# Attention with a mixture of experts on one Trainium2 core: products three periods behind the scores instead of four, with four buffers for the blocks that TensorE turns

## The chip, the cores and the metric

The kernel runs on one core of a Trainium2 chip. The metric is the device time of one execution in microseconds. The kernel before took 584.26 us, the median of three runs (584.21 to 585.72).

## The reference

The input x has 2 batches of 1024 tokens with 128 features, in f32. It is layer-normed, and the output is x plus an attention branch plus a mixture-of-experts branch, both of the normed x:

```python
q = xn @ wq.T                      # 16 heads of 64
lat = xn @ w_down.T                # 64 latent features, shared by all heads
k, v = lat @ w_k_up.T, lat @ w_v_up.T
q, k = rope(q), rope(k)
probs = softmax(q @ k.T / 8 + causal)      # [2, 16, 1024, 1024]
attention = (probs @ v) @ wo.T
```

The experts are 16 of width 64, of which each token uses four (chosen by groups), and one shared expert of width 256.

## The kernel before, in words

All five engines have programs written out by hand, with semaphores between them. The kernel has a first part (layer norm, routing, experts, up to about 126 us) and then the attention loop, which is what the change touches.

**Units and periods.** A unit is one batch and four heads (8 units, `UNITS`). Each unit has 8 periods, so there are 64 (`GRPS`). Period k deals with one pair of heads (a = 0 and 1) and two row blocks of 128 queries: a long one (8, 7, 6 or 5 key blocks) and a short one (1, 2, 3 or 4 key blocks). The two together are always nine key blocks. The work of a period is spread over iterations of the loops `for k in range(-1, GRPS + LAG + 1)`, which every engine runs in its own form. In what follows, iteration i is the pass of that loop with k = i.

**TensorE**, in iteration i, does in this order:
- `long_scores(i + 1)`: scores of the long rows of the next period,
- `project(i - LAG - 1)`: 8 small matmuls that take the products of a period to the 128 output features,
- `turn_slow(i)`: 8 transposes of those probability blocks that TensorE turns itself,
- `rotary`: one piece of q or k for a later unit,
- `short_scores(i + 1)`,
- `products(i - LAG)`: 36 matmuls, latent rows by turned probabilities.

With `LAG = 4` the products of period k stand at the end of iteration k + 4.

**Two ways to turn the probabilities.** The products need each 128x128 block of probabilities transposed. The first five blocks of each long row (`FAST = 5`) are turned by VectorE in 32x32 squares (`turn_fast`, tile `zig`) and then put in place by DMA (tile `fastT`). The other four blocks per head (`SLOW = 4`) are turned by TensorE (`turn_slow`) and copied by ScalarE from PSUM to one of `SLOTS = LAG + 1` buffers `slowT` (`copy_slow`, which waits for the products of period k - SLOTS).

**The exchange.** The DMAs that put the squares in place are issued by SyncE for two periods at a time, pair j being periods 2j and 2j + 1. `exchange(j)` waits until VectorE has turned both periods, and until the products of period 2j - 3 are done, so that the buffer `fastT[j % 2]` is free; it then issues 16 DMAs of 80 KB:

```python
sp.wait_ge(zig_done, 4 * j + 4)
if j >= 2:
    sp.wait_ge(pv_done, 2 * (j - 1))
```

SyncE reaches `exchange(j)` in its own loop at k = 2j + 1. The same queue also issues `stack(n, p)`, 4 DMAs of 256 KB that bring the rotated q and k of unit n into place: `stack(n, 0)` in front of the exchange of k = 8n - 3 (pair 4n - 2), and `stack(n, 1)` in front of the exchange of k = 8n - 1 (pair 4n - 1). The first half of the output is stored by the same queue, at k = GRPS // 2 + LAG + 3.

**Who waits for the exchange.** `products(k)` waits for `in_fast`, the landing of all 16 DMAs of its pair. For an even period k = 2j this is the first use of the pair. On TensorE, everything of the next iteration is queued behind that wait. `turn_fast` on VectorE waits for the exchange of two pairs earlier before it writes over `zig`.

**ScalarE**, in iteration i, does `scale_rows(i - LAG - 1)`, the exponentials of the long rows of i + 1, `copy_slow(i)`, `copy_output(i - LAG)` and the exponentials of the short rows of i + 1. **GpSimd** adds the scaled result of period i - LAG - 1 to the accumulator and rotates q and k.

Of the kernel before, what the change touches and what calls it, by code (L numbers as in the profile page):

```python
# [29 lines left out]

LONG, SHORT = [7, 6, 5, 4], [0, 1, 2, 3]
RING = 8
LAG = 4
SLOTS = LAG + 1
PAIRS = 2
GRPS = 4 * PAIRS * UNITS
# [51 lines left out]
def block_kernel(nc, x, wq, w_down, w_kup, w_vup, wo, gate, e_up, e_down, s_up, s_down,  # L88
                 c_rope, c_ident, c_mask, c_sel, c_lower, out):
    ctx = ExitStack()  # L90
    with ctx:
# [115 lines left out]
        def _(sp):  # L207
# [22 lines left out]
            def exchange(j):  # L230

                s = j % 2
# [3 lines that stand above are left out]
                for turn_ in range(4):  # L236
                    for qi in range(4):
                        ki = (qi + turn_) % 4
                        sp.dma_start(fastT[s][32 * ki:32 * ki + 32, qi],  # L239
                                     zig[s][32 * qi:32 * qi + 32, ki]).then_inc(in_fast[s], 16)  # L240
# [6 lines left out]
            for k in range(-1, GRPS):  # L247
# [8 lines left out]
                if k >= 0 and k % 2:  # L256
                    exchange(k // 2)
                if k == GRPS // 2 + LAG + 3:
                    sp.wait_ge(ad_done, GRPS)
# [9 lines left out]
        def _(pe):  # L269
# [120 lines left out]
            def long_scores(k):  # L390
                if k:
                    pe.wait_ge(max_done, 4 * k)
                if k % 4 == 0:
                    pe.wait_ge(in_qk[pair_of(k)], STACK * (unit_of(k) + 1))
                for chunk in range(2):
                    scores(k, 0, chunk)
# [32 lines left out]
            def project(k):  # L429
                m0 = unit_of(k) % QUADS * 2 + pair_of(k)  # L430
                pe.wait_ge(o_done, k + 1)
                pe.wait_ge(rope_dve, min(k + LAG + 1 + LATER, PIECES * UNITS))
                for c in range(2):
                    for a in range(2):
                        half = slice(HD * a, HD * a + HD)
                        last = nc.tensor.matmul(ps[:, 7 - a, c * P:(c + 1) * P],  # L436
                                                oT[k % 2][half, c * P:(c + 1) * P], mix[half, m0, :],
                                                start=True, stop=True)
                        if c == 1:
                            last.then_inc(proj_pe, 1)  # L440
# [32 lines left out]

            for k in range(-1, GRPS + LAG + 1):
                if 0 <= k and k + 1 < GRPS:
                    long_scores(k + 1)
                if k >= LAG + 1:
                    project(k - LAG - 1)
                if 0 <= k < GRPS:
# [424 lines left out]
```

## Time and profile before

| | |
|---|---|
| median of three runs | 584.26 us |
| the profiled execution | 588.68 us |
| its span, first to last instruction | 586.9 us |
| mean granted TensorE clock, of full speed | 0.971 |
| TensorE matmul busy | 537.9 us (92%) |
| VectorE busy | 407.8 us (69%) |
| ScalarE busy | 398.0 us (68%) |
| GpSimd busy | 194.0 us (33%) |
| moved by DMA | 66.52 MB, mean 113 GB/s |
| DMAs of the exchanges | 512 of 80 KB, 2.1 us from issue to landing (median) |
| DMAs of the stacks | 64 of 256 KB, 4.3 us |

Times within the profile are counted from the first instruction of the profiled execution. A busy share is an average over the whole span; the views by stretch and by time tell what an engine does in one stretch. SPq is the queue of SyncE: its rows are the issuing of DMAs, the transfer itself comes after.

### The profile page before, as it was taken

Reading aid. Unit: us, or ns where it says so; the run is one execution under the profiler, and the core shown is the slowest. Engines: PE = TensorE matmul, PEld = TensorE weight load, DVE = VectorE, ACT = ScalarE, POOL = GpSimd, SP = SyncE. Lnnn points to the kernel's source line nnn. Section 1 sums busy time; section 2 is a strip of 40 time slices with the busy share of each in tenths; the row PEclk is TensorE's granted clock in tenths of the full one; section 3 lists DMA queues with packets and bytes.
Section 4 is the critical chain, followed back from the end, with each engine's and each line's share of the span. In section 5 each row is a group of like instructions: output and inputs, shape, how many; then the busy total and the mean of one; then the engine's idle time right before and its main releaser. Section 6 shows DMA issues by size and latency. Waiting matters only on the chain.

```text
span 586.9 us, 13821 instructions
## 1 busy us (share of the span) xinstructions
PE 537.9 (92%) x4914; PEld 395.9 (67%) x4914; DVE 407.8 (69%) x921; ACT 398.0 (68%) x1036; POOL 194.0 (33%) x271
## 2 busy tenths in 40 slices
PE   3899999986899999999999999999999999898864
PEld 2657776753477777777777777777777776666663
DVE  5495537358877887878788878878877887676400
ACT  2364222347577887888788788878877888888722
POOL 3004404001144443344443344433443432122121
PEclk9599999998899999999999999999999999999977
DMA  9400004202366447646654764466556646654331
GB/s 280 119 1 2 0 1 94 50 2 61 96 157 164 112 99 162 152 108 142 154 138 113 162 163 120 97 151 154 150 137 154 145 118 158 156 126 118 96 86 36
DMA packets 41620, 66.52 MB, mean 113 GB/s; under 512 B 13632, under 2 KB 20688, under 8 KB 41424
## 3 DMA queue, kind: packets, MB, share of 16 engines
q1 hardware_dynamic: 38992, 64.20, 45.8%
q10 hardware_dynamic: 2560, 1.45, 0.8%
q8 instruction: 39, 0.64, 0.5%
q14 instruction: 29, 0.24, 0.1%
HBM read 5.84 MB, written 1.05 MB: 12 GB/s over the span
## 4 chain that ended last, share of the span: by engine, by line
PE 73%; DVE 10%; SPq 7%; issue 5%; ACT 3%; DMA 1%; DVEq 0%; POOLq 0%; POOL 0%; ACTq 0%
PE ps L386 23%; PE ps L425 21%; DVE prob_l L772 6%; SPq L239 6%; PE ps L410 5%; PE ps L451 5%; PE ps L469 4%; PE ps L332 3%; PE ps L436 3%; PE ps L302 1%; PE ps L453 1%; DMA acc<-x 1%; SPq L227 1%; PE ps L348 1%; PE ps L367 1%
## 5 line engine op out<-in xcount | busy, mean ns | idle before, releaser
L772 DVE CUSTOM_DVE_ANT_0 prob_l<-ps,mask 128x1024 f32<-128x1024 f32 (+3 forms) x128 | 126.0, 1022 | 86.7 <-PE ps L386 86.7
L386 PE MATMUL ps<-qk 64*128 64x512 f32 (+3 forms) x768 | 161.1, 524 | 19.8 <-DVE negmax L772 18.6
L593 ACT ACTIVATE prob_l<-prob_l,negmax 128x1024 f32<-128x1024 f32 (+3 forms) x128 | 126.1, 999 | 14.7 <-DVE negmax L772 14.7
L855 POOL TENSOR_TENSOR acc<-acc,scaled 128x256 f32<-128x256 f32 x128 | 93.4, 730 | 124.9 <-ACT scaled L496 119.9
L846 POOL TENSOR_TENSOR roped<-prod 128x256 f32<-128x256 f32 x64 | 46.5, 727 | 221.3 <-DVE prod L663 221.3
L386 PEld LDWEIGHTS ps<-qk 64*128 64x128 f32 x768 | 64.1, 187 | 79.7 <-issue 44.5
L785 DVE STREAM_TRANSPOSE zig<-prob_l 128x640 f32<-128x640 f32 x128 | 100.2, 821 | 1.4 <-DMA fastT<-zig 1.4
L496 ACT ACTIVATE scaled<-ps,rden 128x128 f32<-128x128 f32 x256 | 73.0, 368 | 41.6 <-PE ps L436 41.6
L425 PEld LDWEIGHTS ps<-fastT,lat 128*64 128x64 f32 x1280 | 70.6, 139 | 32.7 <-issue 31.0
L425 PE MATMUL ps<-fastT,lat 128*64 128x128 f32 x1280 | 86.4, 282 | 5.6 <-ACT scaled L496 5.6
L663 DVE TENSOR_TENSOR prod<-ps,rope 128x1024 f32<-128x1024 f32 x64 | 76.7, 1198 | 0.0
L593 ACT ACTIVATE prob_s<-prob_s,negmax 128x128 f32<-128x128 f32 (+3 forms) x128 | 70.1, 551 | 0.1
L496 ACT ACTIVATE slowT<-ps 128x512 f32<-128x512 f32 x128 | 69.6, 606 | 0.0
L425 PE MATMUL ps<-slowT,lat 128*64 128x128 f32 x1024 | 69.3, 279 | 0.0
L425 PEld LDWEIGHTS ps<-slowT,lat 128*64 128x64 f32 x1024 | 60.6, 141 | 0.0
L496 ACT ACTIVATE oT<-ps 128x256 f32<-128x256 f32 x64 | 24.5, 383 | 49.5 <-PE ps L425 49.5
L772 DVE CUSTOM_DVE_ANT_0 prob_s<-ps,mask 128x128 f32<-128x128 f32 (+3 forms) x128 | 56.0, 472 | 2.5 <-PE ps L386 2.5
L410 PE MATMUL ps<-ident,prob_s 128*128 128x128 f32 x320 | 53.5, 276 | 0.7 <-ACT prob_s L593 0.7
L570 ACT ACTIVATE hid<-ps 128x512 f32<-128x512 f32 x32 | 19.1, 597 | 50.1 <-PE ps L453 50.1
L436 PEld LDWEIGHTS ps<-mix,oT 64*128 64x128 f32 x512 | 37.3, 187 | 15.5 <-issue 6.6
L792 DVE TENSOR_TENSOR hid<-hid,ps 128x512 f32<-128x512 f32 x32 | 22.0, 687 | 36.4 <-ACT hid L570 36.3
L847 POOL TENSOR_TENSOR roped<-prod 128x256 f32<-128x256 f32 x64 | 46.5, 726 | 0.0
(121 smaller groups left out, 604.8 us busy)
## 6 DMA issues: line engine op xcount, KB each, us to landing
fastT<-zig SPq DMA_DIRECT2D x512, 80.0 KB, 2.1
qk<-roped SPq DMA_DIRECT2D x64, 256.0 KB, 4.3
acc<-x SPq DMA_DIRECT2D x2, 512.0 KB, 5.6
rope<-c_rope SPq DMA_DIRECT2D x1, 1024.0 KB, 11.2
out<-acc SPq DMA_DIRECT2D x2, 512.0 KB, 3.5
wq_raw<-wq ACTq DMA_DIRECT2D x1, 512.0 KB, 6.7
wo_raw<-wo ACTq DMA_DIRECT2D x1, 512.0 KB, 7.7
sel_raw<-c_sel SPq DMA_DIRECT2D x1, 512.0 KB, 7.1
```

Source lines behind the costliest of these rows:

```text
L386: mm = nc.tensor.matmul(to, qk[p][half, 0, rows], qk[p][half, 1, lo:hi], start=True, stop=True)
L410: last = nc.tensor.transpose(ps[:, 4 + a, n * P:(n + 1) * P], row_sb(k, r + a)[:, kb * P:(kb + 1) * P], ident[:])
L425: last = nc.tensor.matmul(to, lat[:, first + kb, :], probs, start=(at == 0), stop=(at == len(turned) - 1))
L436: last = nc.tensor.matmul(ps[:, 7 - a, c * P:(c + 1) * P], oT[k % 2][half, c * P:(c + 1) * P], mix[half, m0, :], start=True, stop=True)
L496: return nc.scalar.activation(dst, src, ACT.Copy, scale=scale)
L593: nc.scalar.activation(row, row, ACT.Exp, bias=negmax[:, col:col + 1], scale=-1.0, accum_out=den[:, col:col + 1]).then_inc(exp_done, 1)
L663: nc.vector.tensor_tensor(prod[:, e % 2], halves_.unsqueeze(2).broadcast_to([P, 2, 2, QW]), rope[:, :, quarter(e)].unsqueeze(1).broadcast_ ...
L772: nc.vector.tensor_tensor_reduce(row_sb(k, r), row_ps(k, r), mask[:, S - width:], -1.0, 3e38, ALU.add, ALU.min, accum_out=negmax[:, col:co ...
L785: nc.vector.transpose(zig[k // 2 % 2][:, :, k % 2, a].rearrange("p c b n -> p b c n"), row_sb(k, a)[:, 0:FAST * P].rearrange("p (b c n) -> ...
L846: nc.gpsimd.tensor_tensor(to[:, 0, :], x1[:, 0, :], x2[:, 1, :], ALU.subtract)
L847: nc.gpsimd.tensor_tensor(to[:, 1, :], x2[:, 0, :], x1[:, 1, :], ALU.add).then_inc(rot_done, 1)
L855: nc.gpsimd.tensor_tensor(rows, rows, scaled[k % 2][:, a], ALU.add).then_inc(ad_done, 1)
```

## The change

One constant. `SLOTS` follows from it (four `slowT` buffers instead of five), and so do the offsets `LAG` and `LAG + 1` in the loops of TensorE, ScalarE and GpSimd, their number of iterations, and the place of the first output store in SyncE's loop. The products of period k now stand at the end of iteration k + 3, and its projection in iteration k + 4.

```diff
-LAG = 4
+LAG = 3
 SLOTS = LAG + 1
```

The number of `zig` and `fastT` buffers (two each), the places of the exchanges and stacks in SyncE's loop, and the waits in them are as before.

## Rows read from the trace of the kernel before

**Rows 1.** The page: busy time of TensorE, and the granted clock in 40 slices.
```profile
PE 537.9 (92%) x4914; PEld 395.9 (67%) x4914; DVE 407.8 (69%) x921; ACT 398.0 (68%) x1036; POOL 194.0 (33%) x271
PEclk9599999998899999999999999999999999999977
```

**Rows 2.** Stretches: start:end length, busy of each engine, clock, DMA share, GB/s.
```profile
269.20:323.60 54.40, 53.59 (x546) 39.88 (x548) 44.26 (x97) 44.46 (x122) 22.97 (x32) 1.00 0.59 138
```

**Rows 3.** The waits of SyncE's queue: line waited for, us in total, times, longest.
```profile
SPq L239 <- DVE zig L785: 38.7, 2, 35.0
SPq L235 <- PE ps L425: 21.1, 11, 3.3
```

**Rows 4.** Instructions in order of time, VectorE: start, us, what; periods 19, 21, 25.
```profile
259.70 1.56 DVE L785 STREAM_TRANSPOSE zig<-prob_l 128x640 f32<-128x640 f32 x2
...
272.45 1.57 DVE L785 STREAM_TRANSPOSE zig<-prob_l 128x640 f32<-128x640 f32 x2
...
299.90 1.57 DVE L785 STREAM_TRANSPOSE zig<-prob_l 128x640 f32<-128x640 f32 x2
```

**Rows 5.** In order of time, SyncE's queue: exchanges 9 to 12 and two stacks.
```profile
262.54 10.95 SPq L239 DMA_DIRECT2D fastT<-zig  x16
273.52 3.36 SPq L227 DMA_DIRECT2D qk<-roped  x4
276.99 11.74 SPq L239 DMA_DIRECT2D fastT<-zig  x16
288.78 3.17 SPq L227 DMA_DIRECT2D qk<-roped  x4
292.05 12.19 SPq L239 DMA_DIRECT2D fastT<-zig  x16
304.34 10.94 SPq L239 DMA_DIRECT2D fastT<-zig  x16
```

**Rows 6.** Exchanges: KB, median us from issue to landing; then exchange 12's extremes.
```profile
fastT<-zig SPq DMA_DIRECT2D x512, 80.0 KB, 2.1
...
DMA to landing us min/median/max: 2.0/2.1/3.5
```

**Rows 7.** In order of time, TensorE: where products of 17, 19, 20, 21, 23 begin.
```profile
273.80 1.31 PE L425 MATMUL ps<-fastT,lat 128*64 128x128 f32 x20
...
287.61 1.31 PE L425 MATMUL ps<-fastT,lat 128*64 128x128 f32 x20
...
294.43 1.31 PE L425 MATMUL ps<-fastT,lat 128*64 128x128 f32 x20
...
300.88 1.31 PE L425 MATMUL ps<-fastT,lat 128*64 128x128 f32 x20
...
314.30 1.31 PE L425 MATMUL ps<-fastT,lat 128*64 128x128 f32 x20
```

**Rows 8.** SyncE's queue, other exchanges: 0, 14, 15, 18 and 19.
```profile
138.58 10.06 SPq L239 DMA_DIRECT2D fastT<-zig  x16
...
330.11 11.30 SPq L239 DMA_DIRECT2D fastT<-zig  x16
...
344.83 12.15 SPq L239 DMA_DIRECT2D fastT<-zig  x16
...
385.19 12.25 SPq L239 DMA_DIRECT2D fastT<-zig  x16
...
400.76 12.42 SPq L239 DMA_DIRECT2D fastT<-zig  x16
```

**Rows 9.** In order of time, TensorE: end of iteration 3, start of iteration 4.
```profile
150.85 0.49 PE L386 MATMUL ps<-qk 64*128 64x128 f32 x4 [0.97 <-DVE negmax L772]
152.73 1.83 PE L386 MATMUL ps<-qk 64*128 64x512 f32 x4 [1.39 <-DVE negmax L772]
```

**Rows 10.** The chain that ended last, near its end: start, us, what.
```profile
553.81 2.20 PE ps L425 x36
...
556.47 0.76 PE ps L436 x8
...
558.58 3.56 PE ps L425 x36
...
564.71 2.20 PE ps L425 x36
...
575.88 3.79 PE ps L425 x36
```

**Rows 11.** Stretches, columns as in Rows 2: the start of the drain.
```profile
559.30:562.50 3.20, 2.83 (x28) 2.42 (x24) 0.00 (x0) 0.34 (x1) 0.29 (x1) 0.50 0.53 130
```

## The prediction

> **What bounds the kernel now.** I read the page first: TensorE is busy 92% of the span at nearly full clock, and the slices of the granted clock are lower only early and at the end [rows 1]. The stretches then show where the 8% lies: in one whole unit of the attention loop TensorE is busy 53.6 of 54.4 us, at full clock, with VectorE and ScalarE at 44 [rows 2]. So in the loop TensorE is the bound, period for period (6.8 us), and anything that TensorE has to wait for there is added to the time in full. At the end it is no bound but one link of a chain: products, copy, projection, scaling, one after another [rows 10].
>
> The next view is the order of time on SyncE's queue [rows 5], because the change shortens the time in which its exchanges must land. It shows a queue that is nearly full. Between 262.54 and 303 us it issues almost without a break: an exchange is 16 DMAs and takes 10.95 to 12.19 us to issue, a stack 3.2 to 3.4. Four exchanges and two stacks are 52.4 us of a unit's 54.4. The waits say the same: only 11 of the exchanges waited for products to free a buffer [rows 3]; most of the rest found the queue late.
>
> TensorE never waits for an exchange before. How far it is from that follows from two more views, the ends of VectorE's square transposes, which release an exchange [rows 4], and the starts of the products that use it [rows 7]. An exchange has landed 1.5 us after its last issue (2.1 us from issue to landing, less the 0.6 of the issue) [rows 6]. Exchange 10 lands at 276.99 + 11.74 + 1.5 = 290.2 and its products start at 294.43: 4.2 us to spare. Exchange 11 lands at 292.05 + 12.19 + 1.5 = 305.7; its products start one pair (12.9 us) after 294.43, at 307.3: 1.6 us to spare. The change takes a whole period, 6.8 us, from both.
>
> **The change, part by part.**
>
> *The deadline.* products(2j) moves to the slot in which products(2j - 1) stood. What it gives back: before, an exchange waits for the products of period 2j - 3, which stood at the end of the very iteration whose transposes release it. Now these stand one iteration earlier, so the exchange starts at the end of the transposes. For exchange 9 this is 259.70 + 1.56 = 261.3 instead of 262.54, 1.2 us. Nothing is gained where the queue is late anyway. I follow the unit of [rows 4, 5, 7] with the new deadlines, with all times as before it and issue times as measured:
>
> - Exchange 9: starts 261.3, + 10.95 + 1.5 = lands 273.8. Deadline: slot of products 17, 273.8. No wait.
> - The stack in front of exchange 10: 272.3 + 3.4 = 275.7. Exchange 10 starts 275.8, + 11.74 + 1.5 = 289.0. Deadline: slot of products 19, 287.6. TensorE waits 1.4 us.
> - The stack in front of exchange 11: 287.6 + 3.2 = 290.8. Exchange 11 starts 290.9, + 12.19 + 1.5 = 304.6. Deadline: slot of products 21, 300.88, now 302.3 with the first wait. TensorE waits 2.3 us.
> - Exchange 12: the transposes end at 299.90 + 1.57 + 1.4 = 302.9, the queue is free at 303.1; 303.1 + 10.94 + 2.9 (the slowest landing, 3.5 less 0.6 [rows 6]) = 317.0. Deadline: slot of products 23, 314.30 + 3.7 = 318.0. No wait.
>
> So this unit loses 3.7 us: a wait in front of each of the two exchanges that a stack precedes, and the loss is not made good, since TensorE is the bound. It recurs with the next stacks, because the wait delays the next scores and so the next transposes as well. The same working with the issue times of the other units gives 3.1, 2.4, 4.6, 3.7 and 4.1 us for the other five places with both stacks; the smallest is exchanges 14 and 15, with 11.30 and 12.15 us of issuing, the largest 18 and 19, with 12.25 and 12.42 [rows 8]. With 1.0 us at exchange 3 and 2.3 at exchange 30, whose landing is late, the sum is 24.9 us. Behind the waiting products on TensorE are the long scores of the next period, and with them everything.
>
> The bounds of this term: with every exchange at the 10.06 us of exchange 0 [rows 8] it would be 2 us or less; if the waits and delays add up so that no loss at one exchange relieves the next, the waits of the worked unit are 1.4 + 3.7 = 5.1, and the sum some 34.
>
> *The fill.* Iteration 3 gets products that it didn't have. Exchange 0 lands at 138.58 + 10.06 + 1.5 = 150.1, short scores end at 150.85 + 0.49 = 151.3, so they don't wait; they take 2.2 us [rows 10] and end at 153.5, where the next long scores began at 152.73 after 1.39 us of idling [rows 9]. Cost: 0.8 us. Iteration 4 gets a projection, at most 0.8 us [rows 10]. Together + 1.6 us (from 0.8 to 3.0, all of both uncovered).
>
> *The drain.* After the last scores four steps of the chain remain, from products 59 to products 63: 575.88 - 553.81 = 22.07 us, or 5.5 each. One goes. The single steps are 4.8 us (553.81 to 558.58) and 6.1 (558.58 to 564.71), the longer one with products of 3.56 instead of 2.20 at half clock, 1.2 GHz [rows 10, 11]. I take - 5.5 (from - 4.8 to - 6.4). The last exchange doesn't delay it: its squares are turned with period 63, and its products, period 62, still have three steps in front of them or their like.
>
> *Four slowT buffers.* copy_slow(k) waits for the products of period k - 4, before k - 5. Both stand at the end of iteration k - 1, the same place in the order: 0 us. The same holds of the waits of projection, scaling and adding, whose distance from the products is unchanged, and of the first output store, which SyncE reaches one exchange earlier: one DMA of 0.6 us of issuing, in front of exchange 19 instead of 20. It could add its 0.6 us to that wait, the cost is inside the rounding.
>
> **The sum:** + 24.9 + 1.6 - 5.5 = + 21.0 us. Against the profiled execution's 588.68 that is 609.7; the median is 4.4 us lower than the profiled one, so I put the same difference on it: 584.26 + 21.0 = 605.
>
> A rule that speaks against this: the Trainium skill ("DMA: Bandwidth & Descriptors", section "Anatomy of one DMA") prices a DMA at about 2.0 us fixed plus bytes by 436 GB/s. If the 16 DMAs of an exchange (1.31 MB) ran side by side at that price they would have landed 5.0 us after the first issue, every deadline would hold, and the time would fall; that is rival 1. The rows bear out the 2 us of one DMA, but not that the exchange costs no more: the queue needs 10.06 us at the least to issue it.
>
> **The rivals.**
>
> 1. *The exchanges are in time anyway; the change only takes a step off the drain.* For it: TensorE waits for none now, and the queue's measured issue times may stretch only as far as there is room. Against: 10.06 us is the least in any of them, and the stacks in front are fixed work. Its time: 584.26 + 1.6 - 5.5 = 580. It decides if the exchanges behind stacks take under 10.3 us to issue. This is the side of faster. Chance 0.09.
> 2. *The queue is quicker outside the profile.* Single issues of 1.2 to 1.7 us, beyond the two right behind each stack, are much of the 10.9 to 12.2. If only those two slow ones (1.3 us together) stay, exchange 9 takes 10.0, 10 and 11 take 11.3: exchange 10 lands at 287.6, just in time, exchange 11 at 302.3 against 300.9, a wait of 1.4 to 1.5. Six places by 1.5, and 3.3 for exchanges 3 and 30, are 12.3; + 12.3 - 3.9 gives 592.7. For it: the median is 4.4 us under the profiled time. Against: in TensorE's bound loop that difference can lie anywhere. Chance 0.20.
> 3. *The waits cost the clock.* In the drain TensorE fell to 1.2 GHz after gaps of 0.4 and 1.4 us, and a group of products took 1.36 us longer for it (3.56 against 2.20) [rows 10, 11]. Were each wait at the second exchange behind a stack (seven of them) followed by that: + 9.5 us, 614.5. A loss of clock after the first one is largely taken from the second wait. The Trainium skill ("TensorE: Matmul & The Clock Gate", section "HAM oscillation") describes the same pattern for waits on DMAs; its gaps are longer than these 1.4 to 2.6 us. Chance 0.13.
> 4. *Partial relief cancels the drain's gain* (waits of 2 to 6 us in all). Chance 0.05, within 0.3% of before.
>
> **How the numbers follow.** The forecast has 0.53. The range reaches from a little under rival 2 to rival 3: 588 to 615. What is left out is rival 1 and 4 (0.14) and the ends of the others. The forecast's own range is 598 to 611. Slower by over 0.3% (what a measurement of this kernel can tell from none, 1.8 us): 0.53 + 0.20 + 0.13 = 0.86. Within it 0.05, faster 0.09.
>
> **What the profile after would show.** TensorE's first products of even periods wait for a DMA, with 12 to 16 such waits of 1 to 2.6 us, 15 to 25 us in all, at exchanges 4n - 2 and 4n - 1; SyncE's queue no longer waits for products; the unit's stretch is 57 to 59 us instead of 54.4, with 53.6 of TensorE work; the drain has three steps. I am wrong in the mechanism if TensorE waits for no exchange, and in the size if the exchanges take another time to issue, or if the clock row shows 0.5 inside the loop. The likeliest mistake is the size.

## The result

The changed kernel takes 615.1 us, the median of four runs (608.75 to 617.86), against 584.99 for the kernel before: 4.94% slower (ratio 1.0494, 95% interval 1.0435 to 1.0553). The forecast was 605, slower, with a range of 588 to 615; the measured time lies on its upper edge. The profiled execution took 615.48 us, its span is 613.7, where before had 588.68 and 586.9: 26.8 us more. Below, a median is that of all executions of a kernel, and a ratio leaves out those that lie over 1.5% above its fastest.

From the page of the changed kernel, the busy times and the granted clock in 40 slices; they answer to [rows 1]:

```profile
PE 543.5 (89%) x4914; PEld 402.0 (66%) x4914; DVE 407.8 (66%) x921; ACT 397.6 (65%) x1036; POOL 194.0 (32%) x271
PEclk9599999998999999999999999999999899899997
```

VectorE, ScalarE and GpSimd do the same work in the same time. TensorE has the same 4914 matmuls, but 5.6 us more in them, and slices of 8 now stand inside the loop, where before had none.

In order of time, TensorE, at the first products of exchanges 10 and 11; answers to [rows 7]:

```profile
294.14 1.31 PE L425 MATMUL ps<-fastT,lat 128*64 128x128 f32 x20 [0.42 <-issue]
...
309.05 1.31 PE L425 MATMUL ps<-fastT,lat 128*64 128x128 f32 x20 [1.56 <-ACT slowT L496]
```

SyncE's queue in the same unit; answers to [rows 5]:

```profile
267.34 10.40 SPq L239 DMA_DIRECT2D fastT<-zig  x16
...
277.78 3.31 SPq L227 DMA_DIRECT2D qk<-roped  x4
281.20 11.38 SPq L239 DMA_DIRECT2D fastT<-zig  x16
...
292.62 3.18 SPq L227 DMA_DIRECT2D qk<-roped  x4
295.89 11.36 SPq L239 DMA_DIRECT2D fastT<-zig  x16
...
308.03 11.23 SPq L239 DMA_DIRECT2D fastT<-zig  x16
```

Read them together with the landings in the trace. Exchange 10 is issued until 292.58 and has landed 1.5 us later, at 294.05; its products start at 294.14. Exchange 11 is issued until 307.25 and has landed at 308.96; its products start at 309.05. TensorE starts 0.09 us after the exchange is there, and so it does at 20 of the 32 exchanges, all 14 behind a stack among them. Yet neither row names the DMA: the waits are put down to "issue" and to ScalarE's slowT copy. For the whole kernel, what TensorE's matmuls and weight loads on fastT sat idle for, in us and times (both engines' rows are counted, so a wait can stand in it twice):

```profile
  issue: 41.6, 54
  ACT slowT L496: 37.4, 17
  DMA fastT<-zig: 3.0, 2
  ACT scaled L496: 2.8, 2
```

Products wait for three things at once, and most of these rows name one that had come before. That ScalarE was not it is shown once more by a run (below).

The waits of SyncE's queue, answers to [rows 3]:

```profile
SPq L239 <- DVE zig L785: 77.2, 13, 35.4
SPq L235 <- PE ps L425: 3.3, 3, 1.6
```

It waits for transposes 13 times instead of 2, and for a free buffer 3 times instead of 11. That part of the change did what the prediction said: exchanges start at the end of the transposes.

Stretches of the changed kernel: from the products of period 1 to those of period 59, then four falls to half clock inside it (length, busy of each engine, clock, DMA share, GB/s):

```profile
158.00:580.00 422.00, 388.64 (x3904) 289.71 (x3904) 307.75 (x688) 319.48 (x871) 153.61 (x214) 0.98 0.54 128
...
367.30:370.70 3.40, 3.40 (x33) 3.07 (x30) 0.00 (x0) 0.26 (x1) 1.39 (x2) 0.50 0.54 132
411.70:415.00 3.30, 3.30 (x35) 2.97 (x30) 0.07 (x1) 0.00 (x0) 1.41 (x2) 0.50 1.02 242
428.80:432.10 3.30, 3.30 (x31) 2.97 (x29) 0.09 (x1) 0.26 (x1) 1.41 (x2) 0.50 0.40 95
486.80:490.10 3.30, 3.11 (x30) 3.14 (x32) 0.16 (x1) 0.00 (x0) 1.40 (x2) 0.50 0.54 133
```

A fifth lies at 531. In the first of these stretches TensorE is idle for 33.4 us and busy for 388.64.

One thing on counts, for all that follows: the trace has two records for each of the program's f32 matmuls in scores, products and projection. The "36 matmuls" of a period's products are 18 calls, and "16 on slowT and 20 on fastT" are 8 and 10; a transpose has one record.

### The profile page after: what moved, and what is told of

It reads as the page before. It is cut to its first block, busy times and chain, and to the rows that moved or that the text cites. A ratio compares the mean times of both kernels' runs of the same rounds, so it can differ in the third digit from the quotient of the medians.

```text
span 613.7 us, 13824 instructions
## 1 busy us (share of the span) xinstructions
PE 543.5 (89%) x4914; PEld 402.0 (66%) x4914; DVE 407.8 (66%) x921; ACT 397.6 (65%) x1036; POOL 194.0 (32%) x271
## 4 chain that ended last, share of the span: by engine, by line
PE 73%; DVE 9%; ACT 7%; issue 6%; SPq 3%; DMA 1%; DVEq 0%; POOLq 0%; ACTq 0%; POOL 0%
PE ps L386 23%; PE ps L425 23%; DVE prob_l L772 5%; PE ps L410 5%; PE ps L451 5%; PE ps L469 4%; PE ps L332 4%; PE ps L436 3%; SPq L239 3%; ACT prob_l L593 2%; ACT scaled L496 2%; ACT slowT L496 1%; PE ps L302 1%; PE ps L453 1%; DMA acc<-x 1%
## 5 line engine op out<-in xcount | busy, mean ns | idle before, releaser
L425 PE MATMUL ps<-fastT,lat 128*64 128x128 f32 x1280 | 90.2, 290 | 29.1 <-ACT slowT L496 15.6
L425 PEld LDWEIGHTS ps<-fastT,lat 128*64 128x64 f32 x1280 | 74.2, 144 | 56.8 <-issue 34.1
L425 PE MATMUL ps<-slowT,lat 128*64 128x128 f32 x1024 | 72.5, 286 | 0.0
L425 PEld LDWEIGHTS ps<-slowT,lat 128*64 128x64 f32 x1024 | 64.0, 146 | 0.0
```

The costliest lines, as they stand in the source:

```text
L425: last = nc.tensor.matmul(to, lat[:, first + kb, :], probs, start=(at == 0), stop=(at == len(turned) - 1))
```

## The experiments

All were timed in the same sessions as the kernel before, whose median was 584.7 to 587.1 us there. Theory E is that of the prediction: the exchanges land late behind the stacks.

**Five slowT buffers again.**

```diff
-SLOTS = LAG + 1
+SLOTS = LAG + 2
```

Expected: 

> LAG = 3 with five slowT buffers, as before the change. Theory E (exchanges land late behind the stacks on SyncE's queue, and TensorE waits in front of the products of even periods): the number of slowT buffers is nothing to it, the time stays at 609 to 618 us, with about 23 us of waits in front of products of even periods. Rival S (the waits that the profile puts down to ScalarE's slowT copies are real: with four buffers copy_slow is late): the waits go, the time falls to 575 to 592 us.

Measured: 615.37 us (608.59 to 616.09), ratio 1.0472 (1.0391 to 1.0553), as the changed kernel. In its trace, on fastT again:

```profile
  ACT slowT L496: 34.5, 16
```

The loop sits idle for 33.8 us, the changed kernel's for 33.4. So the fourth buffer costs nothing, and the profile's naming of ScalarE is no cause: with a spare buffer the same waits carry the same name, and the products again start 0.09 us after the landing. Rival S falls.

**The matmuls on slowT first.** The wait for the exchange stands between the 16 matmuls on slowT and the 20 on fastT.

```diff
-pe.wait_ge(in_fast[s], SWAPS * (k // 4 + 1))
...
-turned = [fast blocks] + [slow blocks]
+turned = [slow blocks] + [fast blocks]
...
+    if at == SLOW:
+        pe.wait_ge(in_fast[s], SWAPS * (k // 4 + 1))
```

Expected: 

> LAG = 3; within each period's products the 16 matmuls on slowT come first, and only then the wait for the exchange and the 20 matmuls on fastT. Theory E: each deadline moves back by the 1.0 us of those 16 matmuls. The queue's lateness adds up from the first to the second exchange behind stacks, so a unit boundary gains 1.0 us and not 2.1: 7 to 9 us less in waits, and perhaps one or two losses of clock less; 602 to 609 us. Rival S: the products still start with slowT, nothing is gained, 612 to 618 us.

Measured: 608.29 us (598.37 to 612.56), ratio 1.0258 (1.0152 to 1.0365). With nothing else left to wait for at this place, the profile names the cause. First what matmuls and weight loads on fastT sat idle for, then the stretch of the same 58 steps:

```profile
  DMA fastT<-zig: 38.0, 24
...
153.90:566.70 412.80, 386.59 (x3907) 284.17 (x3904) 307.86 (x690) 319.57 (x871) 153.75 (x214) 0.99 0.55 131
```

It sat idle for 26.2 us in the loop instead of 33.4: 7.2 less, inside the 7 to 9 expected, and not the 14 or so that a gain of 1.0 at every wait would be. Two exchanges behind stacks share one backlog. This trace is of the fastest of the four executions, 598.37 us: its span is 17.1 us shorter than the changed kernel's, but the loop gives only 9.2 of that, and 4.1 lie before the loop begins. The four times spread by 14 us, so how much this version gains is known only roughly; that it gains is clear, since its ratio and the changed kernel's (1.0435 to 1.0553) do not overlap.

**The stacks issued by GpSimd**, with LAG = 3 and with LAG = 4.

```diff
-sp.dma_start(qk[p][...], roped[...])
+nc.gpsimd.dma_start(qk[p][...], roped[...])     # in GpSimd's loop, after its rotation; waits left out
```

Expected: 

> LAG = 3; the stacks are issued by GpSimd instead of SyncE, whose queue then holds the exchanges alone. Theory E: an exchange starts when its squares are turned and has 12.5 us until its deadline, against 10.1 to 11 us of issuing and 1.5 us of landing; waits of 0 to 5 us in all remain, and the 6 us of fill and drain show: 579 to 587 us. Rival S, or a rival by which the exchanges are late for their own length and not for the stacks: 605 us or more.

> LAG = 4, the kernel before, with the stacks issued by GpSimd. Theory E: no exchange was late, so nothing is gained: 583 to 587 us. If the stacks on GpSimd by themselves give or cost time, it shows here, and the run of LAG = 3 is to be read against this one.

Measured: 642.69 us with LAG = 3 (ratio 1.0973, 1.0886 to 1.106) and 614.59 with LAG = 4 (1.049, 1.0399 to 1.0581). Both expectations missed: with LAG = 4 this version is itself 27 us slower than the kernel before. With LAG = 4, TensorE in order of time where the first stack is needed, and SyncE's queue while the next is in flight:

```profile
177.27 3.68 PE L377 MATMUL ps<-qk 64*128 64x512 f32 x8 [2.25 <-DMA qk<-roped]
...
186.08 13.98 SPq L241 DMA_DIRECT2D fastT<-zig  x16
```

GpSimd reaches the stack at 169.57, SyncE had it at 162.84; the scores then wait for it (16.2 us in 6 waits), at half clock behind the wait. And exchange 3, with no stack in front of it on its own queue, takes 13.98 us to issue instead of 10.7. So it is at all 14 exchanges that meet a stack: 13.0 to 15.1 us, where before had 10.5 to 12.4. My assumption that a stack costs an exchange only its place in the queue was wrong: while a stack's 1 MB is being moved, the issuing of the exchange is slowed from another queue too. How that splits between the DMA engines and the queue was not settled.

The pair still says something about LAG: LAG = 3 is 28 us slower than LAG = 4 here too. In its trace TensorE waits 2.7 to 3.5 us for each of the exchanges 3, 7, 11, 15, 19 and 23, which took 13.7 to 14.1 us to issue, 6.6 for exchange 26, and under 0.8 for four others; with LAG = 4 it waits in the loop for exchange 26 alone, 1.6 us. That fits late exchanges, but not the claim that the place behind a stack makes them late: by this pair alone it could be their own length, the rival that the expectation names. The changed kernel's own trace speaks to that: of the 25.6 us that its products wait up to exchange 30, beyond the 0.2 and 0.4 that lie there anyway, 23.5 are at the 14 exchanges behind stacks. The others have little to spare: at 5, 17, 25 and 29 TensorE waits up to 0.7 us, at 30 it waits 1.1.

**Twelve of sixteen DMAs**, with LAG = 3 and with LAG = 4.

```diff
-for turn_ in range(4):
+for turn_ in range(0 if j < 2 else 1, 4):
```

The counts that TensorE and VectorE wait for are lowered to match (not shown). The kernel leaves out part of its work, so part of the probabilities is stale; it serves for its time alone.

Expected: 

> LAG = 3; from the third pair on, an exchange issues 12 of its 16 DMAs: the four squares that stay on their own partitions are left as the first two pairs brought them, so that part of the probabilities is stale. Nothing else is changed. Theory E: an exchange then takes 7.6 to 9 us to issue, with 12.5 us from its squares to its deadline, so even behind a stack it lands in time: no waits, no loss of clock in the loop, and what is left is the gain at fill and drain, 6 us: 577 to 582 us where before is 585. Rival (the products three periods behind cost time by themselves): it stays above before.

> LAG = 4 with the same 12 DMAs, the same part of the probabilities stale. Theory E: its exchanges were in time already, so it runs like before, within 2 us. The difference between this and LAG = 3 with 12 DMAs is what fill and drain give: 5 to 7 us.

Measured: 579.74 us with LAG = 3 (575.46 to 581.49), ratio 0.9901 (0.9865 to 0.9937); 583.22 with LAG = 4, ratio 0.9985 (0.9945 to 1.0024). The first is in its range, the second within 2 us of before; the difference is 3.5 us by the medians and 4.9 by the ratios, under the 5 to 7 expected. The loop with LAG = 3 is the yardstick for the others:

```profile
156.40:545.90 389.50, 379.50 (x3906) 281.54 (x3906) 307.82 (x688) 319.87 (x871) 154.06 (x214) 1.00 0.49 115
```

Clock 1.00 throughout, no wait for an exchange, 10.0 us idle. Against it the changed kernel's 422.0 us are 32.5 more: 23.4 more idle, and 9.1 more busy with the same matmuls.

**TensorE kept busy in the waits**, 20 matmuls and then 6.

```diff
+for n in range(BUSY):
+    nc.tensor.matmul(ps[0:HD, 6, 0:P], lat[:, first, :], slowT[...], start=True, stop=True)
 pe.wait_ge(in_fast[s], SWAPS * (k // 4 + 1))
```

Expected: 

> LAG = 3 as changed, but in front of the wait for the exchanges 4n - 2 and 4n - 1 TensorE does 20 matmuls of 128 columns (1.2 us) whose result is overwritten. Theory C (the waits cost 23 us and the falls to 1.2 GHz after them another 6 to 9): the matmuls lie in waits that are there anyway, the granted clock stays at full through the loop, and the time falls by 3 to 8 us, to 607 to 612. Rival (the clock follows from something else, or costs nothing because it only moves into the next wait): no change, or slower by what of the matmuls finds no wait, 614 to 620 us.

> As the kernel with 20 matmuls in front of the waits, but with 6: those took 0.21 us each and not 0.06, 4.2 us in each place, and made the waits vanish under them. Six are 1.26 us; in the trace of the changed kernel the waits at these 14 places were 0.2 to 2.8 us, eleven of them 1.3 or more, so they cost about 2 us in all. Theory C (five or so falls to 1.2 GHz in the loop, 1.7 us each, follow the waits): the granted clock stays at full in the loop and the time falls by 3 to 8 us against the changed kernel's 615, to 607 to 612. Rival: no gain, 615 to 619 us.

Measured: 645.12 us with 20 (ratio 1.1015, 1.094 to 1.109), 616.16 with 6 (1.0503, 1.0454 to 1.0552). The first failed as an experiment: its matmuls took 4.2 us in each place, more than the waits. The second missed its range as well and lies in the rival's (615 to 619), but its loop shows why:

```profile
158.00:579.00 421.00, 401.50 (x4072) 301.19 (x4068) 307.59 (x688) 319.37 (x871) 153.62 (x214) 1.00 0.54 128
```

The clock is 1.00 here, with one fall instead of five. Idle over the yardstick is 9.5 us, busy 22.0, most of it the added matmuls: waits and added work together are some 30 us against 23.4 of waits before, and that ate what the clock gave back. With 20, no fall lies in the loop. So falls of the clock go when the gaps are filled, at no net gain. How firmly is another matter: these are single traces, and the run with five buffers, whose gaps are as the changed kernel's, has three falls in the same 58 steps and not five. In time alone the run decides nothing.

**The kernel before with a delay**: six small DMAs in front of each exchange 4n - 1.

```diff
+for i in range(EXTRA):
+    sp.dma_start(spare[:, i], rope[0:32, 0, 0:128])
```

Expected: 

> LAG = 4, the kernel before, with six small DMAs (0.6 us of issuing each, 3.8 us) in front of each exchange 4n - 1. Theory E: TensorE waits where 3.8 us is more than the exchange had to spare in the trace before (3.9, 2.2, 1.6, 2.9, 0.7, 1.0, 1.0 us): 0 + 1.6 + 2.2 + 0.9 + 3.1 + 2.8 + 2.8 = 13.4 us, and 0 to 7 us for the clock: 597 to 606 us. Rival (lateness on SyncE's queue is absorbed by other slack): within 3 us of before.

Measured: 611.56 us (609.03 to 613.17), ratio 1.0445 (1.039 to 1.0501). Slower as expected, and by more. The six DMAs took 5.0 us where I had put 3.8, and a second engine waits. SyncE's queue, TensorE behind the wait, and VectorE in the same iteration:

```profile
239.19 5.04 SPq L263 DMA_DIRECT2D spare<-rope  x6
...
256.36 1.31 PE L433 MATMUL ps<-fastT,lat 128*64 128x128 f32 x20 [1.30 <-ACT slowT L504]
257.48 1.07 PE L433 MATMUL ps<-slowT,lat 128*64 128x128 f32 x16
259.20 1.13 PE L394 MATMUL ps<-qk 64*128 64x512 f32 x4 [0.65 <-DVE negmax L780]
...
256.37 1.57 DVE L793 STREAM_TRANSPOSE zig<-prob_l 128x640 f32<-128x640 f32 x2 [2.73 <-DMA fastT<-zig]
```

With LAG = 4, VectorE needs the same exchange landed in the same iteration, before it writes over the squares, so its next maxima are late too, 0.65 us here. From the products of period 1 to those of period 59 TensorE has 17.8 us more idle time than before and, with the clock at half for 13.7 us, 6.5 us more of busy time. With no change of LAG at all, the kernel before loses time as soon as seven of its 32 exchanges are late.

**Half a stack moved back.** The matmuls on slowT first, and two of the four DMAs of stack (n, 1) in front of exchange 4n instead of 4n - 1.

```diff
-    stack(n, 1)
+    stack(n, 1, (0,))
...
+if k >= 8 and (k - 1) % 8 == 0:
+    stack(n, 1, (1,))
```

Expected: 

> LAG = 3, the matmuls on slowT first, and of the stack (n, 1), whose rows are needed latest, two DMAs in front of exchange 4n - 1 and two in front of exchange 4n instead of all four in front of the first. Theory E, by the same working as in the prediction with deadlines 1.0 us later: 8.7 us of waits in all instead of 17; 4n has room left that 4n - 1 has not. 586 to 596 us. Rival (a stack costs the same wherever it stands): as with the slowT matmuls first alone, 602 to 612 us.

Measured: 589.52 us (581.41 to 591.09), ratio 1.0008 (0.994 to 1.0077). No more than before, and by the ratios 2.5%, some 15 us, faster than with the slowT matmuls first alone. TensorE's waits for exchanges as the profile counts them, in its slowest execution (591.09 us):

```profile
PE ps L429 <- DMA fastT<-zig: 6.1, 7, 1.7
```

So the place of a stack matters, since the same DMAs are issued in both. The same working that gave 25 us for the change gave 8.7 here, against 6.1 measured: the right order.

**GpSimd copies the squares that stay on their partitions**, so that an exchange is 12 DMAs and the result is whole, with LAG = 3 and LAG = 4.

```diff
-for turn_ in range(4):
+for turn_ in range(1, 4):
...
+for q in range(4):                               # GpSimd, each period; waits left out
+    rows = slice(32 * q, 32 * q + 32)
+    nc.gpsimd.tensor_copy(fastT[s][rows, q, k % 2], zig[s][rows, q, k % 2]).then_inc(diag_done, 1)
```

Expected: 

> LAG = 3, and the squares that stay on their own partitions are copied by GpSimd, four copies of 32 x 320 elements a period, instead of four DMAs of each exchange; the result is whole. Theory E: the exchange is as short as in the kernel that left these DMAs out, which ran at 580 us; if the four copies (0.5 to 1.0 us each, 2 to 4 us of the 3.9 that GpSimd has free in a period of 6.8) fit in, 577 to 584 us, faster than before. If they don't, GpSimd, behind whose copies the rotation and the adding are queued, becomes the bound: over 600 us.

> LAG = 4, the kernel before, with the squares that stay on their own partitions copied by GpSimd. It tells what of the gain of that version (579 us against 585) is the copying and what the change of LAG. Theory E: before had no exchange late, so the shorter exchanges give it nothing: 582 to 587 us, 3 to 6 us above the same with LAG = 3. Rival (the copying itself is the gain): 577 to 581 us, no difference to LAG = 3.

Measured: 579.15 us with LAG = 3 (577.69 to 581.49), ratio 0.9878 (0.9826 to 0.9929), 1.2% faster than the kernel before; 587.11 with LAG = 4 (580.21 to 588.73), ratio 1.0025 (0.9985 to 1.0066), no change that can be told. The second is just above its 582 to 587, and the difference of 8.0 us (1.5% by the ratios) is more than the 3 to 6 expected, where the pair before had 3.5: the size of the gain is known only as some 3 to 9 us. The copies' group on the page, and the same 58 steps of the loop, which agree with the yardstick within 0.02 us on every engine but GpSimd:

```profile
L881 POOL COPY fastT<-zig 32x320 f32<-32x320 f32 x256 | 114.3, 446 | 28.8 <-issue 10.5
...
158.30:547.80 389.50, 379.52 (x3906) 281.56 (x3905) 307.84 (x688) 319.87 (x871) 258.84 (x448) 1.00 0.49 114
```

The change of LAG is a gain once its exchanges are in time: in both pairs the interval of LAG = 3 lies wholly under that of LAG = 4.

## Why the prediction was right, and where it was short

*The bound and the mechanism.* Right. TensorE waits in front of even products for exchanges that stand behind stacks, and the same step backwards is slower with a whole queue and faster with a shorter one.

*The deadline term, 24.9 us.* Right in size: the loop has 23.4 us more idle time than the yardstick, and the waits sit at the exchanges behind stacks. In the worked unit I had 1.4 and 2.3 us; the trace has 0.5 and 1.6 (0.69 and 2.04 us from the start of the last matmul of the scores to the products, less the 0.20 and 0.41 that lie there in the yardstick). The other terms miss by as much, one way and the other. Exchange 2 was put at nothing and waits 1.6 us, since it took 12.56 us to issue and not the 10.47 of before. Exchanges 14 and 15 were put at 2.4 together and wait 3.7, and exchange 30, whose late landing did not come again, waits 1.1 instead of 2.3. That these cancel in the sum to within 1.5 us is luck; the issue time of a single exchange was not to be had to better than 1 or 2 us.

*The clock.* This is the term that was missing. I had made it a rival with chance 0.13, to be added only if it came; it came, five times, and belonged in the sum. The 9.1 us more of busy time with the same matmuls are 1.8 for each fall; in the run with five buffers three falls go with 5.5 us, 1.8 each again. The mistake was to price the waits and then let the granted clock of a loop without waits stand: [rows 2] showed full clock because there was nothing to drop it, while [rows 10, 11] showed the price of gaps of this size. A likelier forecast by my own terms would have been 605 + 5 to 9.5. Rival 3's time of 614.5 is all but the measured one; its size for the clock was right (9.5, from seven falls at 1.4), its rule was not (three of the five falls are at the second exchange behind a stack, two at the first). That the total came so near owes something to the other misses, below. Which gap is followed by a fall is not regular: waits of 2.5 us at exchange 7 had none, one of 2.3 at exchange 15 had. That the number of falls differs between kernels with the same waits may be a part of the spread from 608.75 to 617.86; it wasn't tested.

*The fill, + 1.6.* Wrong in sign, small. The products of iteration 4 start at 157.9, before at 158.67: 0.8 us earlier, of which 0.3 are there already when exchange 0 is issued (138.29, before 138.58). TensorE fell to half clock there in both, but once instead of twice.

*The drain, - 5.5.* From iteration 63's products to the end, before 586.9 - 553.8 = 33.1 us, after 613.7 - 586.2 = 27.5: - 5.6. One clause in it was wrong: the last exchange does hold up the drain. The chain that ended last, near its end:

```profile
594.21 2.06 DMA fastT<-zig
...
596.37 3.66 PE ps L425 x36
...
602.60 3.87 PE ps L425 x36
```

It cost 0.6 us: 2.3 us from the start of the last projection matmul to the products, where the step after has 1.7.

*Four slowT buffers, 0 us.* Right, by the run with five.

*The whole,* in the profiled executions: - 0.8 (fill) + 33.2 (loop, of which 24 waits and 9 clock) - 5.6 (drain) = + 26.8, which is the difference of the spans. The sum of + 21.0 was 5.8 short of that: 8.3 too little for the loop, 2.4 too much for the fill. The other 4.3 of the 10.1 us between 605 and 615.1 come from a step that was no mechanism at all: I carried over that the median lies 4.4 us under the profiled execution, and the changed kernel's lies 0.4 under it. Against its own kind, 609.7 to 615.48, the forecast was nearer than it looks.

*The rivals.* Rival 1 had nearly the right account of what would be left without waits: 580, against the 579.15 of the last version. Rival 2 is out: its queue that is quicker outside the profile would have given 592.7, and the median of 615.1 is hardly lower than the profiled 615.5. The Trainium skill ("DMA: Bandwidth & Descriptors", "Anatomy of one DMA") fits its rule of 2.0 us and bytes by 436 GB/s on DMAs issued by GpSimd, which the prediction did not say; taken over to SyncE's queue as an estimate it would have the 16 DMAs there in 5.0 us, and the trace has 10.0 to 12.7 us of issuing alone. The Trainium skill ("TensorE: Matmul & The Clock Gate", "HAM oscillation") describes a clock that falls at every one of its longer DMA waits; the trace agrees in part, with five falls at some 16 waits.

## What to carry to other kernels

Before a stage is brought nearer to its producer, write down for each transfer when it can start, how long its queue takes to issue it with all that stands in front, and the new deadline; one period's slack on average is not slack behind the other users of the queue. When the sum has waits of one or two microseconds on TensorE, put the clock that follows into it, as a term. A deadline missed can be cured by less issuing (579.15 us here) where moving the other transfers to another queue made it worse. And compare profiled with profiled, median with median: the distance between the two is no constant of a kernel (4.4 us before, 0.4 after).

## What the runs showed that I had not expected

- DMAs issued from another queue lengthened the exchange's issuing: 13.98 us with a stack of 1 MB in flight from GpSimd, 10.7 for the same exchange behind a stack on its own queue.
- Behind a stack on SyncE's own queue, the first two DMAs of an exchange took about 1.2 us each to issue instead of 0.59 (1.17 and 1.23 in exchange 10 of the changed kernel).
- The added matmuls of 128 columns took 0.21 us each, which is two records of 0.11 us (20 calls are 40 records, 6 are 12); the products' 36 records of the same size take 2.12 us, 0.06 each. By those, 20 calls would have been 2.4 us and not the 1.2 of the expectation: 1.2 of the 3.0 us missed were a miscount. For the rest the trace has this: records of products start in pairs, 0.007 us apart, and a pair every 0.109 us, while the added ones start singly, one every 0.109. By the program, products alternate between two halves of 64 partitions of PSUM and the added ones all go to one. The projection, which alternates too, starts in pairs though each of its matmuls begins and ends a sum of its own. So the halves are the likely cause, but no run changes them alone.
- GpSimd copies 32 x 320 f32 elements in 0.45 us, 114 us in all, beside a loop of the same 389.5 us.
